# Count one-hots of a graph kernel stored chunk by chunk, so that both matmul operands are packed

## The reference

```python
h = jnp.maximum(_layernorm(x, axis=-1), 0.0)
x = x + _L0_gnn_ref(h, edge_index, ...)     # two GAT layers, 4 heads x 512, then 1 head x 768
h = jnp.maximum(_layernorm(x, axis=-1), 0.0)
x = x + _L1_gnn_ref(h, ...)                 # two GCN layers, 768 x 768
```

## Time and profile before

| | us |
|---|---|
| median of 3 runs | 1326.92 (1325.04 to 1327.08) |
| the profiled execution's own time | 1326.07 |
| its span, first to last instruction | 1324.2 |
| PE busy | 1227.1 (93%) |
| DVE busy | 850.8 (64%) |
| ACT busy | 510.6 (39%) |
| mean granted TensorE clock | 0.952 of full speed |

### The profile page before, as it was taken

One profiled execution on the slowest core, in us unless ns is written; L12 is line 12 of the kernel. 1 busy time (PEld: TensorE's weight loads), 2 busy tenths in 40 slices (PEclk: granted clock), 3 DMA queues, 4 the chain that ended last, 5 costly groups with the idle time before them and its releaser, 6 DMA issues. The chain is left out here.

```text
span 1324.2 us, 17459 instructions
## 1 busy us (share of the span) xinstructions
PE 1227.1 (93%) x7119; PEld 1107.6 (84%) x7119; DVE 850.8 (64%) x1372; ACT 510.6 (39%) x1037; POOL 25.5 (2%) x39
## 2 busy tenths in 40 slices
PE   2799999999989999999999999995899999999998
PEld 2576676776779999999999999994799999989998
DVE  7952733647579768876887678857886652351253
ACT  1311212112165555555555565512544552152111
POOL 5000000000010000000000000000000000000000
PEclk9788888889999999999999999997899999999999
DMA  5003021300011020102010201000310220010131
GB/s 189 14 27 96 31 57 64 91 29 25 0 56 49 1 80 1 49 1 80 1 48 1 80 1 49 1 0 13 117 48 25 92 73 1 1 36 0 65 113 58
DMA packets 27618, 58.44 MB, mean 44 GB/s; under 512 B 3492, under 2 KB 6152, under 8 KB 27536
## 3 DMA queue, kind: packets, MB, share of 16 engines
q1 hardware_dynamic: 27344, 56.96, 13.1%
q10 hardware_dynamic: 192, 0.32, 0.1%
HBM read 41.73 MB, written 15.54 MB: 43 GB/s over the span
## 5 line engine op out<-in xcount | busy, mean ns | idle before, releaser
L1250 PE MATMUL banks<-hs,ring_hi 128*128 128x258 f32 (+1 forms) x1600 | 300.7, 289 | 4.0 <-DVE ring_lo L507 2.1
L1250 PEld LDWEIGHTS banks<-hs,ring_hi 128*128 128x128 f32 (+1 forms) x1600 | 249.0, 189 | 5.7 <-issue 2.5
L1250 PE MATMUL banks<-hs,ring_lo 128*128 128x258 f32 (+1 forms) x800 | 227.4, 284 | 0.0
L481 ACT ACTIVATE e<-banks,al 128x256 f32<-128x256 f32 (+1 forms) x500 | 194.0, 491 | 22.4 <-PE banks L466 22.4
L1250 PEld LDWEIGHTS banks<-hs,ring_lo 128*128 128x128 f32 (+1 forms) x800 | 151.4, 189 | 0.0
L489 ACT ACTIVATE ring_hi<-pf 128x512 fp32r<-128x512 f32 (+1 forms) x125 | 81.7, 654 | 158.6 <-DVE pf L500 155.4
L807 DVE TENSOR_TENSOR hot<-codes,parts_of 125x1920 bf16<-125x1920 uint16 x80 | 90.2, 1155 | 78.9 <-PE banks L1147 78.6
L1278 PE MATMUL banks<-w_hi,oT_hi 128*128 128x384 f32 (+1 forms) x320 | 110.3, 345 | 11.3 <-DVE rows L997 5.5
L1134 PE MATMUL banks<-w_hi,xT_hi 128*128 128x512 f32 x240 | 111.7, 466 | 3.5 <-DVE w_lo L801 3.5
L1147 PE MATMUL banks<-hot 125*128 125x160 bf16 x480 | 110.2, 401 | 0.0
L498 DVE TENSOR_TENSOR e<-e 128x512 f32<-128x512 f32 (+1 forms) x125 | 84.5, 676 | 39.1 <-ACT e L481 39.0
(11 more groups left out here) (267 smaller groups left out, 2250.3 us busy)
## 6 DMA issues: line engine op xcount, KB each, us to landing
h_scratch<-stage SPq DMA_DIRECT2D x30, 256.0 KB, 2.0
hs<-h_scratch SPq DMA_DIRECT2D x30, 256.0 KB, 2.9
w_st<-in_L_gnn_W SPq DMA_DIRECT2D x4, 1536.0 KB, 10.2
w_st<-in_L_gnn_W SPq DMA_DIRECT2D x16, 384.0 KB, 3.5
gw_st<-in_L_gnn_W SPq DMA_DIRECT2D x12, 384.0 KB, 3.8
xr<-in_x SPq DMA_DIRECT2D x9, 384.0 KB, 6.8
rows<-in_x SPq DMA_DIRECT2D x9, 384.0 KB, 3.4
x_scratch<-rows SPq DMA_DIRECT2D x9, 384.0 KB
```

The source lines that it names most:

```text
L481: last = nc.scalar.activation(self.e[:, local % 2, a, i, 0:n], self.p_shift[:, a, 0:n], ACT.Exp, bias=scores[a][:, g * G + i:g * G + i + 1])
L1250: last = nc.tensor.matmul(p_a[0:m, dt, half, 0:HH], wt.ring[a][:, s // G, s % G, dt * P:dt * P + m], hs[:, s, b, half * HH:(half + 1) * HH ...
```

## The change

`hot` and `codes` get the chunk index outside the column index, so that the 128 or 160 values that one matmul reads lie side by side. The compare then writes 12 runs (2 one-hots x 6 chunks) of 160 values, in each of which the compared number is the same. To compare in pairs, every low value and every key is stored twice, side by side (the last dimension of `parts_of`, of size 2), and the operand steps over 80 pairs with a stride of 0. `window_parts` writes each of the two copies with a pair of instructions of its own. The number of elements of the compare and of the matmuls stays the same.

```diff
-        self.codes = edges("codes", [EC, 2, WK, FIX], u16)
-        self.parts_of = edges("parts_of", [EC, NW, 2, FIX], u16)
+        self.codes = edges("codes", [EC, 2, FIX, WK], u16)
+        self.parts_of = edges("parts_of", [EC, NW, 2, FIX, 2], u16)
...
-        self.hot = heads("hot", [EC, SLOTS, 2, WK, FIX], bf16)
+        self.hot = heads("hot", [EC, SLOTS, 2, FIX, WK], bf16)
...
-            nc.gpsimd.iota(codes[:, :, :, :], pattern=[[OFFSET, 2], [1, WK], [0, FIX]], base=0, channel_multiplier=0).then_inc(made, 1)
+            nc.gpsimd.iota(codes[:, :, :, :], pattern=[[OFFSET, 2], [0, FIX], [1, WK]], base=0, channel_multiplier=0).then_inc(made, 1)
...
-                chain(nc.vector.tensor_copy(parts_of[:, :, 0, :], s_lo[:, :].rearrange("e (w i) -> e w i", i=FIX)), False)
-                chain(nc.vector.tensor_tensor(parts_of[:, :, 1, :], d_f[:, :].rearrange("e (w i) -> e w i", i=FIX),
-                                              s_hi[:, :].rearrange("e (w i) -> e w i", i=FIX), ALU.add))
+                for twin in range(2):
+                    chain(nc.vector.tensor_copy(parts_of[:, :, 0, :, twin], s_lo[:, :].rearrange("e (w i) -> e w i", i=FIX)), False)
+                    chain(nc.vector.tensor_tensor(parts_of[:, :, 1, :, twin], d_f[:, :].rearrange("e (w i) -> e w i", i=FIX),
+                                                  s_hi[:, :].rearrange("e (w i) -> e w i", i=FIX), ALU.add), twin == 1)
...
-                nc.vector.tensor_tensor(hot[:, wd % SLOTS, :, :, :], codes[:, :, :, :],
-                                        parts_of[:, wd, :, :].unsqueeze(2).to_broadcast([EC, 2, WK, FIX]),
+                nc.vector.tensor_tensor(hot[:, wd % SLOTS, :, :, :].rearrange("e a i (v t) -> e (a i) v t", t=2),
+                                        codes[:, :, :, :].rearrange("e a i (v t) -> e (a i) v t", t=2),
+                                        parts_of[:, wd, :, :, :].rearrange("e a i t -> e (a i) t").unsqueeze(2)
+                                        .to_broadcast([EC, 2 * FIX, WK // 2, 2]),
                                         ALU.is_equal).then_inc(hot_ready, 1)
...
-                    last = nc.tensor.matmul(count_bank(g)[:, at:at + WK], hot[:, wd % SLOTS, 0, 0:P, i], hot[:, wd % SLOTS, 1, :, i],
+                    last = nc.tensor.matmul(count_bank(g)[:, at:at + WK], hot[:, wd % SLOTS, 0, i, 0:P], hot[:, wd % SLOTS, 1, i, :],
```

## The result

| | before | after |
|---|---|---|
| median, us | 1326.69 (1325.04 to 1327.08, 4 runs) | 1230.45 (1226.70 to 1236.01, 4 runs) |
| profiled execution, us | 1326.07 | 1236.01 |
| span, us | 1324.2 | 1234.1 |
| PE / DVE busy | 93% / 64% | 92% / 69% |
| mean granted clock | 0.952 | 0.971 |

The ratio is 0.928, 95% interval 0.924 to 0.932. What failed is a size, the distance between packed count matmuls: I took 85 ns and 80 as the least, and it is 67.5.

The account below looks back on a forecast made before the run. PE was taken to bound the stretch of the counts. Gains of 60.1 + 24.7 + 1.5 less 1.0 make 85.3 us, so the profiled 1326.07 becomes 1240.8 and the median 1241.5 us, range 1236 to 1268.

Parts of the forecast that it names:

- What bounds the kernel: Stretch of the counts, 236.60 us: PE alone sets the pace, while DVE has compares ready early and waits 78.6 us.
- (1) Packed counts: 480 count matmuls on PE: packed reads bring them from 210 to 85 ns apart, gain 60.1 us.
- The rule on weight loads: Rival for count matmuls on PE: the weight load sets their distance at 107 ns, total 1252 us; chance 0.09.
- (2) Clock: 26 tiles between count stretches: PE's clock no longer drops, 111.0 us in place of 135.7, gain 24.7 us.
- Tiles 27 and 28: Two tiles behind the counts: 8.4 us at full clock in place of 9.86, gain 1.5 us.
- (3) Compare: Compare on DVE: stays at two elements per cycle, 1155 ns, and DVE stays barely early enough: 0 us.
- (4) Copies: Writing parts twice on DVE ahead of the `xT_lo` step: one more pair of instructions, loss 1.0 us (0 to 2).
- (5) Behind the counts: Extra round on DVE and later work: one-hots stay covered by tiles 27 and 28, all only moves forward: 0 us.
- the clock still drops: Rival: PE's clock still falls behind count stretches because the matmuls are short, not strided: 1267.7 us; chance 0.13.
- One element per cycle: Rival: the stride-0 operand slows the compare to some 2.25 us, DVE sets the stretch: about 1310 us; chance 0.04.
- Slower, short rows cost a cycle each: Rival: 960 rows of two each cost DVE a further cycle, 3.3 us a compare: about 1387 us; chance 0.03.

Follow-up runs that it names:

- Run 6: The changed kernel with its packed one-hots kept as 4-byte values (fp32r) instead of bf16, and 3 buffers: 1280.82 us, one run.
- run 3: The kernel before with only the moving one-hots packed, the stationary ones still strided, the compare split in two: 1230.27 us, ratio 0.930.
- Run 4: The kernel before, still strided, with the three count windows moved between the k steps of the following tile: 1299.92 us, ratio 0.985.
- the second profile: Profile from running the changed kernel again with no edit: median 1230.88 us, ratio 0.931 against the kernel before.

## Why the prediction was right or wrong

- **What bounds the kernel**: right. PE set the stretch, and DVE's idle time was slack that the change used up.
- **(1) Packed counts**: the mechanism was right, the size was not, and it is the step that put the forecast out of its range: 8.4 of the 11 us. I took 85 ns and a lower bound of 80, by drawing a line through rows of 258 to 512 columns with 4-byte operands. Measured: 67.5 ns, 32.4 us for all 480, a gain of 68.5 and not 60.1. Run 6 shows why those rows were a bad base: one-hots 4 bytes wide are 109 ns apart, bf16 ones 67.5 (the number of buffers also differs, but the stretch shown had no wait). The 12 ns on top of the columns do not apply to bf16, and in 4-byte values at 160 columns there is more on top than 12 ns. A bound taken from another type was no bound. Which of the two 4-byte operands makes the 109 ns is open.
- **The rule on weight loads** (upper end, 107 ns) did not decide here: a distance like it appears only where both operands are 4 bytes wide (run 6), and run 3 shows that even a strided bf16 load hides behind a 160-column matmul.
- **(2) Clock**: right, 24.7 us forecast. The 26 tiles take 142.04 - 32.4 = 109.6 us against 111.0 in my sum (4.22 each, since 4.27 held a slow change-over from the strided counts). Run 4 confirms what I had only read from rows, that the drops come behind an unbroken slow stretch, and puts 23 to 24 us on them, against 24.7 + 1.5 forecast.
- **Tiles 27 and 28**: 1.56 us, forecast 1.5.
- **(3) Compare**: right in the outcome, 1151 ns and no stall of PE. The reason given did not hold to the end: I had DVE's 5.65 us in a step with columns under PE's 5.8, but PE's real step was 5.43, so that DVE fell behind by 0.2 us in each such step. The compares made ahead covered it; nothing waited but weight loads, 2.1 us in all. Had I foreseen the packed distance, I would have had to put a price on this.
- **(4) Copies**: forecast 1.0 us with 2 as the bound; measured 1.3 of DVE's own and PE's wait, and 2.0 up to the first count in the first profile. The repeated pair is not just a second 1.01: all four instructions, which write with a stride of two, were longer; and the last transposes took 0.66 us more at the lower clock, which the sum did not have.
- **(5) Behind the counts**: right. The 4.0 us that the first profile lost there are absent in the second.

For the profiled execution the terms close: 1240.8 forecast, -8.4 (67.5 in place of 85 ns), -1.4 (tiles), -0.1, +1.0 (copies and clock ahead of the counts), +4.0 (that execution's rest) give 1235.9; measured 1236.0. Without that +4.0 the time is 1232.0, which is what the second profile has (1232.03). It is by luck that the profiled execution lies only 5 us from its forecast. No term explains the remaining 1.6 us down to the median of 1230.45, for which I had even added 0.85; single runs spread from 1226.7 to 1236.0.

- **The rivals**: "the clock still drops" fell, by the rows after and by run 4. "One element per cycle" did not happen here, but it is what a version without the copies does: 2149 ns (2.25 us forecast) and 1282 us (1310 forecast). The 1310 was too high because it gave DVE 210 us of work and 10 us of waits in the stretch, and DVE needed 192.03 us and never waited. Of its 1.13 to 1.2 ns per element, hold only the upper end (1548 for 1280). "Slower, short rows cost a cycle each" fell: 960 rows of two ran at the double rate.

## What to carry to other kernels

When a matmul is recorded as longer than its columns explain, look at the stride of its moving operand first: in these runs of 160 bf16 columns a stride of 4 bytes cost 2 ns a matmul and from 6 to 12 bytes the time grew in proportion, while the stationary operand's stride counted for 2 to 7 ns. Take the distance of matmuls only from rows of the same operand width, or treat an extrapolation as no bound at all. And a long slow stretch costs twice, once in itself and once by the clock of what follows: breaking it into pieces of 1.14 us gave back a quarter of the whole gain with no other edit.

## What the runs showed of the hardware that I had not expected

- At the full clock, 160 bf16 values of the moving operand took 104, 140 and 210 ns at strides of 6, 8 and 12 bytes, 9.1 to 9.2 bytes of address range per ns (8.7 to 8.8 by the starts inside a stretch). A stride of 4 bytes is nearly as good as none (69.9 against 67.5 ns).
- A packed bf16 matmul of 160 columns, with a weight load of its own, takes hardly more than its columns: 67.5 ns (69 to 70 inside a stretch), where 160 columns at 2.4 GHz are 66.7. The same in 4-byte values takes 109 ns.
- DVE instructions of 480 elements got 0.1 to 0.2 us longer when they wrote every second 2-byte value.
